# Graph layer on one core: the gather skips rows of edges that belong to another tile

## The reference

```python
msgs = feat[src]
neigh = segment_sum(msgs, dst, num_segments=6250)
rst = (1.0 + eps[0]) * feat + neigh
h = maximum(rst @ W1 + b1, 0.0)        # 512 -> 1024
h = h @ W2 + b2                        # 1024 -> 512
x = layernorm(x + (h + feat))          # feat is x
```

## Time and profile before

| | |
|---|---|
| median of the three runs | 1142.06 us |
| profiled execution, its own time | 1143.88 us |
| its span, first to last instruction | 1141.9 us |
| mean granted TensorE clock | 0.934 |
| PE busy | 980.2 us (86%) |
| POOL busy | 834.8 us (73%) |
| DVE busy | 349.8 us (31%) |
| ACT busy | 254.3 us (22%) |
| DMA engines busy, most slices | 70% to 80% |

### The profile page before, as it was taken

How to read it: one execution, slowest core, us unless ns; L and a number is a source line. 1 busy time by engine, 2 the same in 40 slices (tenths; PEclk the granted TensorE clock), 3 DMA queues, 4 the chain that set the end, 5 groups by cost and what they waited for, 6 DMA issues and landing times.

```text
span 1141.9 us, 17705 instructions
## 1 busy us (share of the span) xinstructions
PE 980.2 (86%) x6234; PEld 627.9 (55%) x6234; DVE 349.8 (31%) x847; ACT 254.3 (22%) x512; POOL 834.8 (73%) x861
## 2 busy tenths in 40 slices
PE   2478988978989989889889889889889889889887
PEld 1144655755655655546556546546547547547556
DVE  4323323323223223222322322332332233232232
ACT  1122222222212212212212212212212122122222
POOL 6777777777777777777777777777777777777740
PEclk9889989999889989889899989899999899899999
DMA  7978787787787787787787777777787877877840
GB/s 221 307 230 237 212 245 233 214 246 231 212 243 226 224 243 220 221 238 218 230 243 219 229 242 218 234 233 214 241 234 211 245 228 211 249 228 215 240 143 19
DMA packets 89797, 255.48 MB, mean 224 GB/s; under 512 B 18679, under 2 KB 21160, under 8 KB 89744
## 3 DMA queue, kind: packets, MB, share of 16 engines
q0 software_dynamic: 68096, 223.01, 66.8%
q1 hardware_dynamic: 21680, 32.22, 8.5%
HBM read 242.34 MB, written 13.62 MB: 224 GB/s over the span
## 4 chain that ended last, share of the span: by engine, by line
POOL 58%; issue 21%; PE 13%; DMA 6%; DVE 1%; POOLq 0%; SPq 0%; ACT 0%; DVEq 0%; ACTq 0%
POOL raw L394 58%; PE hp L912 6%; PE acc L940 5%; DMA raw<-in_x_dram,idx 5%; PE y L928 1%; DMA late<-in_L_gnn_W_dram 1%; DMA xt<-in_dst_dram 1%; DMA rowdst<-in_dst_dram,rowidx 0%; PE tables L865 0%; POOLq L223 0%; PE tables L851 0%; DVE moments L768 0%; DVE late L764 0%; SPq L355 0%; DVE raw L632 0%
## 5 line engine op out<-in xcount | busy, mean ns | idle before, releaser
L394 POOL DMA_INDIRECT raw<-in_x_dram,idx x850 | 830.9, 978 | 260.9 <-issue 253.0
L940 PE MATMUL acc<-raw,onehot 128*32 128x512 f32 x2300 | 321.6, 643 | 128.6 <-DMA raw<-in_x_dram,idx 122.0
L912 PE MATMUL hp<-rstT_hi,w_hi 128*128 128x250 f32 x800 | 243.5, 304 | 4.0 <-DVE rstT_lo L744 4.0
L912 PE MATMUL hp<-rstT_lo,w_hi 128*128 128x250 f32 x800 | 240.2, 300 | 0.0
L912 PE MATMUL hp<-rstT_hi,w_lo 128*128 128x250 f32 x800 | 239.1, 299 | 0.0
L940 PEld LDWEIGHTS acc<-raw,onehot 128*32 128x32 f32 x2300 | 58.3, 111 | 248.6 <-DMA raw<-in_x_dram,idx 147.3
L912 PEld LDWEIGHTS hp<-rstT_lo,w_hi 128*128 128x128 f32 x800 | 168.4, 210 | 20.1 <-issue 20.1
L912 PEld LDWEIGHTS hp<-rstT_hi,w_lo 128*128 128x128 f32 x800 | 166.7, 208 | 20.1 <-issue 20.1
L912 PEld LDWEIGHTS hp<-rstT_hi,w_hi 128*128 128x128 f32 x800 | 167.8, 210 | 5.2 <-DVE rstT_lo L744 4.3
L506 ACT ACTIVATE late<-hp,b1c 128x250 f32<-128x250 f32 x200 | 83.0, 467 | 382.2 <-PE hp L912 382.2
L928 PE MATMUL y<-w_hi,hT_hi 128*125 128x512 f32 x400 | 164.5, 411 | 0.0
(11 more groups left out here) (69 smaller groups left out, 367.3 us busy)
## 6 DMA issues: line engine op xcount, KB each, us to landing
raw<-in_x_dram,idx POOLq DMA_INDIRECT x850, 3.8
xt<-in_x_dram SPq DMA_DIRECT2D x50, 224.0 KB
out_dram<-late SPq DMA_DIRECT2D x50, 224.0 KB
late<-in_L_gnn_W_dram SPq DMA_DIRECT2D x7, 512.0 KB, 6.6
xt<-in_x_dram SPq DMA_DIRECT2D x50, 26.0 KB
out_dram<-late SPq DMA_DIRECT2D x50, 26.0 KB
win<-pad_src SPq DMA_DIRECT2D x52, 8.5 KB
win<-pad_dst SPq DMA_DIRECT2D x52, 8.5 KB
```

Source lines behind the costliest of these rows:

```text
L394: pool.indirect_dma_start(out=raw[:, i, k, :], out_offset=None, in_=table[:, :], in_offset=bass.IndirectOffsetOnAxis(ap=idx[:, slot, k:k + ...
L912: mm = pe.matmul(hp[jp % 2][:, jj, :], w1[a][:, c, j * P:(j + 1) * P], rstT[b][:, half, c, :], start=(c == 0 and term == 0), stop=(c == TC ...
L940: mm = pe.matmul(acc[i][q * QN:(q + 1) * QN, :], onehot[:, i, AT[q] + k - FIRST[q], :], raw[:, i, k, :], start=(k == FIRST[q]), stop=(k == ...
```

## The change

Two things change, for the tiles from the third on (`T` >= 2):

- `window_tables` marks the edges whose `place` is below 0 or at least 125 and adds 1,000,000 (`FAR`) to their `idx`. It takes three more small DVE instructions on 128 x 17 and a memset of one element, each behind a wait on the one before it; `place` is now made first and `idx` last.
- `gather` gives the indirect DMA a bound (`bounds_check=N - 1`, which is 6249) and `oob_is_err=False`: rows whose index is above it are left out and raise no error. Their places in `raw` keep the finite rows of an earlier tile, which the zeros of the one-hot matrix take out of the sum. The first two tiles gather as before, so that both halves of `raw` are filled once.

The bound is handed over in a register, and the built program sets that register again ahead of each of these gathers: one more register move on POOL's sequencer for each of the 16 x 17 gathers of either path's program, of which the path that runs executes 48 x 17 = 816.

```diff
+        apart = sb("apart", [P, 2, SLOTS], F32)
...
+        s_own = sem("s_own")
...
-            def gather(table, i, k, slot, signal):
-                pool.indirect_dma_start(
-                    out=raw[:, i, k, :], out_offset=None, in_=table[:, :],
-                    in_offset=bass.IndirectOffsetOnAxis(ap=idx[:, slot, k:k + 1], axis=0)).then_inc(signal, 16)
+            def gather(table, i, k, slot, signal, skip=False):
+                rows = bass.IndirectOffsetOnAxis(ap=idx[:, slot, k:k + 1], axis=0)
+                if skip:
+                    pool.indirect_dma_start(out=raw[:, i, k, :], out_offset=None, in_=table[:, :], in_offset=rows,
+                                            bounds_check=N - 1, oob_is_err=False).then_inc(signal, 16)
+                else:
+                    pool.indirect_dma_start(out=raw[:, i, k, :], out_offset=None, in_=table[:, :],
+                                            in_offset=rows).then_inc(signal, 16)
...
-                                gather(table, i, k, (res + i) % 4, s_gather[i][b])
+                                gather(table, i, k, (res + i) % 4, s_gather[i][b], not (type(T) is int and T < 2))
...
             def window_tables(T, slot):
+                if type(T) is int and T < 2:
...
+                    return
                 dve.wait_ge(s_winT, T + 1)
-                dve.tensor_copy(idx[:, slot, :], tables[:, 0:SLOTS]).then_inc(s_idx, 1)
                 dve.tensor_scalar(place[:, slot, :], tables[:, SLOTS:2 * SLOTS],
-                                  first_node[:, bass.ds(T, 1)], None, ALU.subtract).then_inc(s_place, 1)
+                                  first_node[:, bass.ds(T, 1)], None, ALU.subtract).then_inc(s_own, 1)
+                dve.wait_ge(s_own, 3 * T - 5)
+                dve.tensor_scalar(apart[:, 0, :], place[:, slot, :], 0.0, None, ALU.is_lt).then_inc(s_own, 1)
+                dve.wait_ge(s_own, 3 * T - 4)
+                dve.scalar_tensor_tensor(out=apart[:, 1, :], in0=place[:, slot, :], scalar=float(TN), in1=apart[:, 0, :],
+                                         op0=ALU.is_ge, op1=ALU.add).then_inc(s_own, 1)
+                dve.wait_ge(s_own, 3 * T - 3)
+                dve.scalar_tensor_tensor(out=idx[:, slot, :], in0=apart[:, 1, :], scalar=FAR, in1=tables[:, 0:SLOTS],
+                                         op0=ALU.mult, op1=ALU.add).then_inc(s_idx, 1)
+                dve.wait_ge(s_idx, T + 1)
+                dve.memset(gone[0:1, 0:1], 0.0).then_inc(s_place, 1)
```

More of the change, by code:

```diff
@@ L606, in window_tables @@
             def window_tables(T, slot):
+                if type(T) is int and T < 2:
+                    dve.wait_ge(s_winT, T + 1)
+                    dve.tensor_copy(idx[:, slot, :], tables[:, 0:SLOTS]).then_inc(s_idx, 1)
+                    dve.tensor_scalar(place[:, slot, :], tables[:, SLOTS:2 * SLOTS],
+                                      first_node[:, bass.ds(T, 1)], None, ALU.subtract).then_inc(s_place, 1)
+                    return
                 dve.wait_ge(s_winT, T + 1)
-                dve.tensor_copy(idx[:, slot, :], tables[:, 0:SLOTS]).then_inc(s_idx, 1)
                 dve.tensor_scalar(place[:, slot, :], tables[:, SLOTS:2 * SLOTS],
-                                  first_node[:, bass.ds(T, 1)], None, ALU.subtract).then_inc(s_place, 1)
+                                  first_node[:, bass.ds(T, 1)], None, ALU.subtract).then_inc(s_own, 1)
[9 more added lines that the diff above has]
+                dve.memset(gone[0:1, 0:1], 0.0).then_inc(s_place, 1)
             def one_hot(i, slot, q, signal):
```

## The result

The changed kernel is slower: 1173.79 us in the median of 4 runs (1172.92 to 1178.17) against 1141.05 us (1139.84 to 1143.20, 4 runs). The ratio is 1.029, with a 95% interval of 1.026 to 1.032. The forecast was 1135 us and faster; what came is the first rival, the bound that costs POOL time in each gather, which was priced at 1176 us. The profiled execution took 1173.82 us, 29.94 more than that of before.

What follows compares the result with a forecast made beforehand. POOL, handing out one gather each 1.25 us, was taken as the bound; -8.5 + 1.1 - 0.5 + 0 + 0 = -7.9 us against 1143.88 gave 1136.0, on the median's footing 1134, predicted as 1135 us, range 1108 to 1217.

Steps and rivals of the forecast that it cites:

- the first rival: On POOL: the bound costs time in each gather, 1176 us at 0.05 us a gather, 1266 at 0.16; chance 0.36.
- the bound itself: In the 816 gathers with a bound on POOL: the register move and the comparison of indices, both taken as 0.
- (b): Inside each gather: comparing 128 indices with the bound, taken as 0, upper end 131 us; decides from 0.010 us a gather.
- Register moves: On POOL's sequencer ahead of each gather with a bound: hidden under the running gather, 0 us, 155 us at worst.
- The DVE chain: On DVE behind the tables: L756 slides by about 0.7 us and stretches fewer gathers, -8.5 us, between -5.4 and -9.7.
- +1.1 for L625: On DVE: the new L625 reads two SBUF operands for 0.17 us and meets 14 of 48 gathers, +1.1 us.
- Fewer rows for POOL: In POOL's gathers: leaving out foreign rows saves 0 us, judged from gathers of 100 rows; strict proportion would save 60 us.
- The third rival: In the gathers of columns 15 and 16: POOL's time follows the rows, 1120 us at a quarter proportion, 1075 at all; chance 0.12.
- Fewer bytes: On the DMA engines: some 17 MB less of 223 MB, 0 us in the loop, 0.5 us gained at the end.
- the forecast's own 1129 to 1142: Whole kernel: the range of the forecast case, with the bound free and a slide gain of 5 to 10 us; chance 0.41.
- The prediction's rule for the stretch: For gathers on POOL begun during a DVE instruction with two SBUF operands: they last longer until 0.12 us before its end.

Runs made afterwards that it cites:

- 7: The changed kernel with 1,000,000 added to every index from the third tile on, so that all 816 gathers fetch nothing: 1170.8 us.

## Why the prediction was wrong

**The step that failed** is "the bound itself", its part (b): "a comparison for each, which is less work than a row, should hardly be seen; that gives 0". It measured 52 ns a gather, 816 x 0.052 = 42.4 us, and the text had said that the term decides from 0.010 us on. Two things were wrong in the reason given. It inferred the price of 128 rows from a gather of 100 rows of another shape, from whose two durations I had subtracted locks (waits for a DVE instruction) by a rule fitted elsewhere; the runs with 64 rows show 0.72 ns a row, so that 28 rows would have been 20 ns, too little to find in those two rows and enough to matter 816 times. And it took the bound for work on each index alone: some 24 of the 52 ns come once for a gather. That a comparison is less work than a row was true (0.22 against 0.72 ns), but 128 of them are 28 ns, nearly three times the point of decision. The first rival's price, 1.00 against 0.95, was right to 2 ns, and its 1176 us to 0.2%, but by luck: the 1.00 was a gather of 100 rows without a bound, and by the prediction's own reading a DVE instruction had held it up by 0.05 us. What was right was that rival's mechanism.

**Register moves: 0.** Right. The gaps stayed at 0.30 us, and with the register set once the time is the same.

**The DVE chain: -8.5, and +1.1 for L625.** Right in mechanism and sign, and small by a third: the forecast allowed up to -9.7, and the stretches beside `double_x` fell by 11.1 us. L777 came 0.91 us behind the tables' first instruction (1.0 forecast), a slide of 0.65 us; the stretches fell by 11.4 us in sum. L625 and L623 stretch nothing: 3 gathers begin during the one and 15 during the other, and none lasts over 3 ns more than 998. The +1.1 was too much by its own rule, too, which leaves 0.17 - 0.12 = 0.05 us for a gather beside L625 and so 0.7 us for 14. The chain alone, without a bound, took 12.4 us off (ratio 0.988), more than the 7.9 that the forecast had for everything together.

**Fewer rows for POOL: 0.** The number holds for rows beyond the bound, but not for the reason given: such a row isn't taken off POOL's list, as the packets show. Rows really left off the gather do shorten it, by 0.72 ns each; for the 8340 foreign rows that would be 6 us and not the 60 of strict proportion. The third rival is out for both reasons: columns 15 and 16 are no shorter than the others.

**Fewer bytes: 0 in the loop, -0.5 at the end.** Right: 206 MB were forecast and 205.9 moved, and with next to no data (7) the loop kept its rhythm. At the end 1.2 us were gained, within the 0 to 1.25 given.

**What was weighed wrongly beyond the term.** The chance of the first rival was 0.36 against 0.41, so the case wasn't ignored; but the upper end of its price in the range, 0.10 us, was kept while the lower end was taken as likeliest, with no run behind either. The measured time lies in the range, on the other side of no change, and outside the forecast's own 1129 to 1142. (The lower end, 1108, is not half of the third rival's proportion, which is 1105.) What the first rival had for it, that the cost falls on the one engine without slack and nothing hides it, should have weighed more than an argument on how small the cost is.

## What to carry to other kernels

Where GpSimd hands out indirect DMAs back to back, count instructions and not bytes: here a gather costs 1.25 us, of which 0.09 us depend on its 128 rows (128 x 0.72 ns), so a bound that spares the rows costs time (52 ns each), while a branch that spares the whole gather gives it back (50 us for 41 gathers). A term of a few nanoseconds must be multiplied by its count before it is called nothing: 0.010 us was the point of decision here. And look at where DVE instructions with two SBUF operands fall against the starts of the gathers: 0.65 us of delay in small instructions was worth 1.2% by itself.

## What the runs showed of the hardware that was not expected

- An index beyond the bound saves no place among the packets: 68,096 in the gathers' queue with none, 8% or nearly all of the rows beyond. Only the bytes (some 4 are left of a row's 2048) and the landing (3.8, 3.5 and 2.1 us) change.
- The bound costs 52 ns with 128 indices and 38 with 64, some 24 ns a gather and 0.22 ns an index; a row costs 0.72 ns, in a gather of 946 ns.
- Where two gathers with a bound stand between fifteen without, the two last 1011 ns (998 to 1002 where all have it) and the next two without one 962 (949 the rest). Why isn't known.
- The prediction's rule for the stretch (end of the DVE instruction less start of the gather less 0.12 us) was read from the kernel before and holds in the changed one: of its stretched gathers beside `double_x`, h_lo and the one-hot matrices, most come within 0.01 us of it.
- POOL's sequencer hides a register move (29 ns), a load from SBUF (0.29 us) and a branch (45 ns) under the gather that runs.
